# Two graph attention layers on one core: layer 1's turned matrix split between TensorE and transposing DMAs

## Chip, core and metric

One Trainium2 chip, one of its cores. The metric is the device time of one execution in microseconds, as the median of the runs shown. The inputs are x (4096 x 128, fp32), an adjacency matrix of 4096 x 4096 int32 with about 0.2% of ones, crowded at low indices, and the weights of the two layers.

## What is computed

```python
# layer 0
h = x @ W
e = leaky_relu((h @ a_src)[:, None] + (h @ a_dst)[None, :], 0.2)
valid = (adj > 0) & (h.sum(axis=1) != 0)[None, :]
att = where(valid, softmax(where(valid, e, -1e9), axis=1), 0)
attention = where(att >= 1e-4, att, 0) * valid.sum(axis=1)[:, None]   # and 0 where a row's top is under 1e-4
x = layernorm(x + elu(h + attention @ h))
# layer 1
scores = where(adj > 0, leaky_relu(x @ ks.T, 0.2), -9e15)
x = layernorm(x + softmax(scores, axis=1) @ ks)
```

Both layers are dense over the 4096 x 4096 pairs. Everything but the loads and stores happens on chip.

## The kernel before

The 4096 rows are cut into 32 tiles of 128 rows, one per partition. A tile's row of the attention matrix has 4096 columns, which are 32 blocks of 128 and 4 chunks of 1024. Nodes' features `h_all`, the row `d_all` of destination terms, `zero_cols`, and ks in several forms stay in SBUF for the whole program.

For one tile, layer 0 runs so. VectorE's `mask0` adds `d_all` to a mask (0 or a huge negative number) and takes the row maximum. ScalarE's `bend0` applies the leaky slope and `raise0` the exponential with its sum, in two halves. VectorE's `cut` zeroes what is below the threshold. TensorE's `turn0` transposes the 32 blocks into PSUM (L290), ScalarE's `copy0` brings them to `att0T`, and `sum0` multiplies them with `h_all` in fp32 (L410). `residual0`, `elu_exp`, `elu` and `normalise0` give the tile x1 of 128 x 128. `turn_q` transposes it (L444) and `q_high_part` and `q_low_part` split it in two fp16 parts.

Layer 1 then: `score` (L381, L382, L386) makes the products of the fp16 parts of q and ks, `bend1` the leaky slope into `att1`, `mask1` adds the mask and takes the maximum, `raise1` the exponential. `turn1` transposes all 32 blocks on TensorE (L290 again). ScalarE's `copy1` writes their fp16 high part, scaled by 1024, to `high1T` (L687), and VectorE's `low_part1` what is left, also fp16, to `low1T` (L996). `sum1` multiplies both with the fp16 parts of ks and a column of ones: two matmuls per block, 257 and 129 columns wide (L438, L439):

```python
pe.matmul(acc, high1T[:, part], k_parts[:, k, 0:2 * D + 1], start=(k == 0), stop=False)
mm = pe.matmul(acc[:, D:], low1T[:, part], k_parts[:, k, D:2 * D + 1], start=False, stop=(k == BLOCKS - 1))
```

`finish1` divides by the sum (L1003), adds the two products (L1005, L1008), and `normalise1` ends the tile.

Masks: POOL's queue loads each adjacency tile twice, with a cast from int32 to bf16. `load_adj` (L1325) fills one of three `mask` buffers for layer 1. For layer 0, SP's queue copies `zero_cols` into one of two `mask_zero` buffers (`lay_zeros`, L265) and `add_adj` (L1329) adds the adjacency tile to it in flight. `build_mask` (L889) and `zero_mask` (L899) turn both into masks.

PSUM has three places of 1024 columns (`work`) that scores and turned blocks share in a fixed rotation, and two banks for the sums. Each engine has its own queue, and its order is written out by hand as a list per slot: slot t holds layer 0's sums of tile t, the turn and part of the sums of layer 1 for tile t-1, and the scores of tile t; `to_first_slot`, `first_slot`, `early_slots` and `last_slots` are the start and the end. Semaphores alone tie the engines together.

## Time and profile before

| | |
|---|---|
| median of 3 runs | 857.0 us (856.76 to 857.24) |
| span of the profiled execution | 855.3 us |
| busy: TensorE / VectorE / ScalarE / POOL | 827.0 / 788.1 / 760.6 / 224.9 us |
| packets of the DMA queues of POOL / SP | 66.06 MB / 38.80 MB |

The profile is of one execution, and its page gives the span, from the first to the last instruction, as that execution's time; it has no second figure. Busy time is the time in which at least one instruction of the engine runs. Matmuls are pipelined, so the duration of one is longer than the distance to the next; what one costs is read from the distances.

### The profile page before, as it was taken

How to read it: one execution, taken by the hardware profiler on the slowest of the kernel's cores; microseconds unless marked ns; L12 is line 12 of the kernel's file. 1: busy time of each engine (PE TensorE's matmuls, PEld its weight loads, DVE VectorE, ACT ScalarE, POOL GpSimd, SP SyncE). 2: the span in 40 equal slices, each digit the busy share in tenths (PEclk: the TensorE clock that was granted, in tenths of full speed). 3: DMA queues.
4: the chain of work that ended last, by engine and by line, in shares of the span. 5: the costliest groups of instructions: out<-in, count | busy, mean ns of one | idle time of the engine just before them, and what ended most of it. 6: DMA issues, size and time to landing. Idle time of an engine off the chain costs nothing.

```text
span 855.3 us, 17732 instructions
## 1 busy us (share of the span) xinstructions
PE 827.0 (97%) x7139; PEld 714.2 (84%) x7139; DVE 788.1 (92%) x1009; ACT 760.6 (89%) x732; POOL 224.9 (26%) x446
## 2 busy tenths in 40 slices
PE   7489999999999999999999999999999999999997
PEld 7468888888998888889888888988888898888876
DVE  3999999999999999999999999999999999997865
ACT  2899999999999999999999999999999999998763
POOL 2033232323312233332223333222233321222100
PEclk9799999999999999999999999999999999999999
DMA  9999786666688766668866667886666678611000
GB/s 212 239 131 172 151 149 102 122 130 131 141 155 148 106 120 130 132 139 154 151 104 122 130 131 139 153 153 104 126 124 136 135 151 155 103 31 24 13 2 10
DMA packets 39969, 106.07 MB, mean 124 GB/s; under 512 B 11088, under 2 KB 23504, under 8 KB 32208
## 3 DMA queue, kind: packets, MB, share of 16 engines
q0 software_dynamic: 20864, 66.06, 53.5%
q1 hardware_dynamic: 18592, 38.80, 12.7%
q8 instruction: 57, 0.93, 0.4%
q14 instruction: 24, 0.20, 0.1%
q10 hardware_dynamic: 432, 0.07, 0.1%
HBM read 138.48 MB, written 2.10 MB: 164 GB/s over the span
## 4 chain that ended last, share of the span: by engine, by line
PE 83%; DVE 9%; ACT 4%; issue 2%; DMA 1%; POOLq 0%; POOL 0%; ACTq 0%; DVEq 0%
PE work L290 23%; PE sums L410 23%; PE sums L438 12%; PE work L381 6%; PE work L382 6%; PE work L386 6%; PE sums L439 6%; DVE att1T L996 2%; DVE att L908 2%; ACT att L677 1%; ACT att L634 1%; PE sums L444 1%; PE work L315 1%; ACT att L654 1%; ACT att0T L666 1%
## 5 line engine op out<-in xcount | busy, mean ns | idle before, releaser
L290 PE MATMUL work<-ident,att 128*128 128x128 f32 x2072 | 256.2, 275 | 14.0 <-DVE att L1098 12.6
L290 PEld LDWEIGHTS work<-ident,att 128*128 128x128 f32 x2072 | 233.6, 142 | 22.7 <-DVE att L1098 13.0
L410 PE MATMUL sums<-h_all,att0T 128*128 128x128 f32 x2048 | 244.2, 275 | 0.0
L410 PEld LDWEIGHTS sums<-h_all,att0T 128*128 128x128 f32 x2048 | 236.1, 192 | 0.1
L438 PE MATMUL sums<-k_parts,att1T 128*128 128x257 f16 x1024 | 182.3, 274 | 0.3 <-DVE att1T L996 0.2
L439 PE MATMUL sums<-k_parts,att1T 128*128 128x129 f16 x1024 | 177.3, 218 | 0.0
L996 DVE SCALAR_TENSOR_TENSOR att1T<-work,att1T 128x1024 f16<-128x1024 f32 x128 | 152.3, 1209 | 12.9 <-ACT att1T L687 12.8
L687 ACT ACTIVATE att1T<-work 128x1024 f16<-128x1024 f32 x127 | 129.4, 1029 | 27.9 <-PE work L290 27.9
L921 DVE SCALAR_TENSOR_TENSOR att<-att,cut 128x2048 f32<-128x2048 f32 x62 | 145.2, 2346 | 0.0
L672 ACT ACTIVATE att<-work 128x1024 f32<-128x1024 f32 x128 | 127.7, 1028 | 19.5 <-PE work L386 19.5
L960 DVE CUSTOM_DVE_ANT_0 att<-att,mask 128x2048 f32<-128x2048 f32 x62 | 141.3, 2282 | 2.0 <-ACT att L672 2.0
L908 DVE CUSTOM_DVE_ANT_0 att<-mask_zero,d_all 128x4096 f32<-128x4096 bf16 x31 | 137.0, 4420 | 1.7 <-PE work L290 1.7
L666 ACT COPY att0T<-work 128x1024 f32<-128x1024 f32 x128 | 126.7, 1023 | 4.5 <-PE work L290 4.5
L677 ACT ACTIVATE att<-att,bias 128x2048 f32<-128x2048 f32 x62 | 126.0, 2036 | 2.6 <-DVE bias L987 2.6
L654 ACT ACTIVATE att<-att,bias 128x2048 f32<-128x2048 f32 x62 | 124.7, 2011 | 0.0
L634 ACT ACTIVATE att<-att,node_parts 128x4096 f32<-128x4096 f32 x31 | 114.9, 3708 | 0.0
L438 PEld LDWEIGHTS sums<-k_parts,att1T 128*128 128x128 f16 x1024 | 100.3, 98 | 14.2 <-issue 0.4
L439 PEld LDWEIGHTS sums<-k_parts,att1T 128*128 128x128 f16 x1024 | 100.4, 98 | 1.3
L381 PE MATMUL work<-kT,qT 128*128 128x512 f16 x256 | 97.7, 382 | 0.9 <-ACT qT L697 0.7
L382 PE MATMUL work<-kT,qT 128*128 128x512 f16 x256 | 97.8, 382 | 0.0
L1325 POOL DMA_DIRECT2D mask<-adj x31 | 19.3, 622 | 226.6 <-DVE top L960 225.4
L386 PE MATMUL work<-kT,qT 128*128 128x512 f16 x256 | 76.6, 381 | 0.0
(123 smaller groups left out, 669.6 us busy)
## 6 DMA issues: line engine op xcount, KB each, us to landing
mask<-adj POOLq DMA_DIRECT2D x31, 1024.0 KB, 8.6
mask_zero<-zero_cols SPq DMA_DIRECT2D x29, 1024.0 KB, 5.0
mask_zero<-adj POOLq DMA_DIRECT2D x29, 1024.0 KB, 11.7
att<-x SPq DMA_DIRECT2D x4, 512.0 KB, 6.7
k_parts<-ks POOLq DMA_DIRECT2D x2, 1024.0 KB, 19.7
x_sb<-x SPq DMA_DIRECT2D x32, 64.0 KB, 2.8
out<-x SPq DMA_DIRECT2D x32, 64.0 KB, 4.8
mask<-adj POOLq DMA_DIRECT2D x2, 512.0 KB, 6.6
```

Of the source, the lines that this page charges most:

```text
L290: mm = pe.transpose(place[:, b * P:(b + 1) * P], source(c * PER + b), ident[:, :])
L381: pe.matmul(o, qT[:, 0, :], kT[:, 0, part], start=True, stop=False)
L382: pe.matmul(o, qT[:, 0, :], kT[:, 1, part], start=False, stop=False)
L410: mm = pe.matmul(acc0, att0T[:, k * P:(k + 1) * P], h_all[:, k, :], start=(k == 0), stop=(k == BLOCKS - 1))
L438: pe.matmul(acc, high1T[:, part], k_parts[:, k, 0:2 * D + 1], start=(k == 0), stop=False)
L439: mm = pe.matmul(acc[:, D:], low1T[:, part], k_parts[:, k, D:2 * D + 1], start=False, stop=(k == BLOCKS - 1))
L666: nc.scalar.copy(att0T[:, cols(c)], work[:, (1, 2, 0, 1)[c], :]).then_inc(copied0, 1)
L677: nc.scalar.activation(att1[:, half(k)], att1[:, half(k)], ACT.Exp, bias=bias1[u % 2][:, :]).then_inc(exp1, 1)
L908: nc.vector.tensor_tensor_reduce(att0[p][:, :], mask_zero[p][:, :], d_all[:, :], 1.0, -NO_ROW_MAX, ALU.add, ALU.max, top0[p][:, :]).then_i ...
L921: nc.vector.scalar_tensor_tensor(b, b, cut0[p][:, :], b, ALU.is_ge, ALU.mult).then_inc(cut_done, 1)
L960: nc.vector.tensor_tensor_reduce(att1[:, half(k)], att1[:, half(k)], mask[u % MASKS][:, half(k)], 1.0, -3.0e38, ALU.add, ALU.max, top1[u % ...
L996: nc.vector.scalar_tensor_tensor(low1T[:, cols(c)], work[:, (2, 0, 1, 2)[c], :], LIFT, high1T[:, cols(c)], ALU.mult, ALU.subtract).then_in ...
```

## The change

It changes layer 1's turn and sums, the masks, some buffers, and the order of all five queues.

1. Of layer 1's 32 blocks, TensorE turns the first 12 (`WHOLE_BLOCKS`), in two fills of 6. ScalarE copies them in fp32, times 1024, to `whole1T`, and `sum_whole` multiplies them in fp32 with `k_whole`, ks and a column of ones, 129 wide.
2. The other 20 are split where they lie, before any turn: ScalarE's `split_high` writes the fp16 high part to a new buffer `high1`, VectorE's `low_part1` the low part in two pieces of 1280 columns into the tail of `att1`. SP issues three transposing transfers per tile (`turn_high`, `turn_low` twice) into `high1T` and `low1T`. `sum_split` multiplies them, one slot later than the whole ones, with three matmuls per block.
3. The last tile uses no transposing transfer: all its blocks are turned by TensorE.
4. The sums of layer 1 are 129 columns in place of 257, so `finish1` has one product less.
5. One adjacency load per tile, in four buffers. `zero_mask` makes layer 0's mask as a minimum of `mask` and `zero_cols`; `lay_zeros` and `add_adj` go.
6. `raise0` is one exponential over 4096 columns in place of two halves.
7. Smaller buffers are shared (`elu0`, `res1`), x1 has three buffers, and all orders are new; the PSUM places follow a table of fills.

```diff
+FILL_BLOCKS = 6
-MASKS = 3
+MASKS = 4
-            def turn1(u, c, layer0):
-                turn(work[:, (2, 0, 1, 2)[c], :], c, lambda b: att1[:, b * P:(b + 1) * P]).then_inc(turned1, 1)
+            def turn1(u, i):
+                blocks = fill_blocks(i)
...
+            def sum_whole(u, i):
+                pe.wait_ge(copied1, 2 * u + i + 1)
...
+                for k in fill_blocks(i):
+                    mm = pe.matmul(acc1, whole1T[:, k * P:(k + 1) * P], k_whole[:, k, :], start=(k == 0), stop=False)
...
+            def split_sum(blocks):
+                for b in blocks:
+                    k = b - WHOLE_BLOCKS
                     part = slice(k * P, (k + 1) * P)
-                    pe.matmul(acc, high1T[:, part], k_parts[:, k, 0:2 * D + 1], start=(k == 0), stop=False)
-                    mm = pe.matmul(acc[:, D:], low1T[:, part], k_parts[:, k, D:2 * D + 1], start=False, stop=(k == BLOCKS - 1))
+                    pe.matmul(acc1, high1T[:, part], k_parts[:, k, 0:D + 1], start=False, stop=False)
+                    pe.matmul(acc1[:, 0:D], high1T[:, part], k_parts[:, k, D + 2:], start=False, stop=False)
+                    mm = pe.matmul(acc1, low1T[:, part], k_parts[:, k, 0:D + 1], start=False, stop=(b == BLOCKS - 1))
...
+            def sum_split(u, i):
...
+                if i == 0:
+                    pe.wait_ge(high_turned, 16 * (u + 1))
+                pe.wait_ge(low_turned[i], 16 * (u + 1))
...
+            def turn_high(u):
+                sp.wait_ge(high_ready, u + 1)
+                if u > 0:
+                    sp.wait_ge(summed1, 4 * u)
...
+                sp.dma_start_transpose(high1T.rearrange("p (b r) -> p b r", r=P), high1[:, :]).then_inc(high_turned, 16)
+            def turn_low(u, i):
+                sp.wait_ge(low1, 2 * u + (1 if i == 1 else 2))
...
+                sp.dma_start_transpose(low1T[:, piece(i)].rearrange("p (b r) -> p b r", r=P),
+                                       att1_halves[:, low_at(i)]).then_inc(low_turned[i], 16)
...
             def slot(t):
-                if t + 4 < TILES:
-                    lay_zeros(t + 4)
...
+                store(t - 4)
+                load_x(t + 1)
+                turn_low(t - 1, 1)
+                turn_low(t - 1, 0)
+                turn_high(t - 1)
...
             def bend1(u, c):
                 act.wait_ge(scored, 4 * u + c + 1)
...
+                    for i in range(2):
+                        if low_at(i).start < 2 * (c + 1) * CHUNK and low_at(i).stop > 2 * c * CHUNK:
+                            act.wait_ge(low_turned[i], 16 * u)
...
+            def split_high(u):
+                act.wait_ge(exp1, 2 * u + 2)
+                if u > 0:
+                    act.wait_ge(high_turned, 16 * u)
+                nc.scalar.activation(high1[:, :], att1[:, WHOLE_COLS:N], ACT.Copy, scale=LIFT).then_inc(high_ready, 1)
...
-                    nc.vector.tensor_scalar(m, m, 0.0, -NO_EDGE, ALU.is_le, ALU.mult).then_inc(zero_masked, 1)
+                nc.vector.tensor_tensor(mask_zero[:, :], mask[f % MASKS][:, :], zero_cols[:, :],
+                                        ALU.min).then_inc(zero_masked, 1)
...
-            def low_part1(u, c):
+            def low_part1(u, i):
+                dve.wait_ge(high_ready, u + 1)
+                if i == 0:
+                    dve.wait_ge(low1, 2 * u + 1)
+                nc.vector.scalar_tensor_tensor(att1_halves[:, low_at(i)], att1[:, piece_cols(i)], LIFT, high1[:, piece(i)],
                                                ALU.mult, ALU.subtract).then_inc(low1, 1)
...
-                    pe.wait_ge(kT_low, c + 2)
+                if t == 0:
+                    pe.wait_ge(kT_low, CHUNKS)
```

How the orders move, at three places of a slot in the middle of the program. In the rows a name without its buffer number stands for the buffer, x8 for eight of the same kind in a row.

TensorE before: layer 0's turns and sums with layer 1's turns between them, then layer 1's sums in pairs (16 blocks, of which two are shown).

```order
L290 MATMUL work<-ident,att_1 128x128 x24
L410 MATMUL sums<-h_all,att0T 128x128 x8
L290 MATMUL work<-ident,att_1 128x128 x8
L410 MATMUL sums<-h_all,att0T 128x128 x16
L290 MATMUL work<-ident,att 128x128 x8
L410 MATMUL sums<-h_all,att0T 128x128 x8
L290 MATMUL work<-ident,att 128x128 x8
L438 MATMUL sums<-k_parts,att1T 128x257
L439 MATMUL sums<-k_parts,att1T 128x129
L438 MATMUL sums<-k_parts,att1T 128x257
L439 MATMUL sums<-k_parts,att1T 128x129
```

TensorE in the change, from layer 0 to the split sums (L391 is `turn0`, L518 `sum0`, L528 `turn1`, L547 to L549 one block of `split_sum`), and below it from the second fill of `turn1` to the next scores (L540 is `sum_whole`, L566 `turn_q`, L494 `score`).

```order
L391 MATMUL work<-ident,att_1 128x128 x32
L518 MATMUL sums<-h_all,att0T 128x128 x32
L528 MATMUL work<-ident,att 128x128 x6
L547 MATMUL sums<-k_parts,att1T 128x129
L548 MATMUL sums<-k_parts,att1T 128x128
L549 MATMUL sums<-k_parts,att1T 128x129
L547 MATMUL sums<-k_parts,att1T 128x129
```

```order
L528 MATMUL work<-ident,att 128x128 x6
L540 MATMUL sums<-k_whole,att1T 128x129 x6
L566 MATMUL sums<-ident,x_0 128x128
L540 MATMUL sums<-k_whole,att1T 128x129 x6
L494 MATMUL work<-kT,qT 128x512
```

Layer 0 stands in one piece, `turn1` has 12 blocks in place of 32, and the split sums of the tile before stand between its two halves; the second half of the whole sums comes behind the turn of q and ahead of the scores.

ScalarE before, from `bend0` (L634) over the cast of q (L697) and one half of `raise0` (L654) to the four `bend1` (L672):

```order
L634 ACTIVATE att_1,absent<-att_1,node_parts 128x4096
L687 ACTIVATE att1T<-work 128x1024
L697 CAST qT<-sums 128x128
L687 ACTIVATE att1T<-work 128x1024
L654 ACTIVATE att_1,z<-att_1,bias 128x2048
L672 ACTIVATE att<-work 128x1024 x4
L666 COPY att0T<-work 128x1024
L654 ACTIVATE att_1,z<-att_1,bias 128x2048
L666 COPY att0T<-work 128x1024 x2
```

and in the change (L893 is `elu_exp`, L820 `bend0`, L876 `copy1`, L899 the cast of q, L840 `raise0`, L863 `bend1`, L851 `copy0`):

```order
L893 ACTIVATE elu<-elu 128x128
L820 ACTIVATE att_0,absent<-att_0,node_parts 128x4096
L876 ACTIVATE att1T<-work 128x768
L899 CAST qT<-sums 128x128
L840 ACTIVATE att_0,z<-att_0,bias 128x4096
L863 ACTIVATE att<-work 128x1024 x4
L851 COPY att0T<-work 128x1024 x4
L868 ACTIVATE att<-att,bias 128x1536
```

The exponential of layer 0 stands whole between the cast of q and the four bends, and the four copies of layer 0 follow in one piece.

VectorE before, from a low part (L996) over `elu` (L937 to L944) and `finish1` (L1003 to L1013) to `normalise0` (L951):

```order
L996 SCALAR_TENSOR_TENSOR att1T<-work,att1T 128x1024
L937 TENSOR_TENSOR low<-y_exp,x_sb 128x128
L939 SCALAR_TENSOR_TENSOR res<-y,low 128x128
L942 BN_STATS stat<-res 128x6
L944 BN_AGGR mv<-stat 128x2
L1003 RECIPROCAL rz<-sums 128x1
L1005 SCALAR_TENSOR_TENSOR res_half<-sums,rz,x 128x128
L1008 SCALAR_TENSOR_TENSOR res<-sums,rz,res_half 128x128
L1011 BN_STATS stat<-res 128x6
L1013 BN_AGGR mv<-stat 128x2
L996 SCALAR_TENSOR_TENSOR att1T<-work,att1T 128x1024
L951 TENSOR_SCALAR x<-res,mv,rstd 128x128
```

and in the change (L1243 is a low piece, L1193 to L1200 `elu`, L1256 to L1265 `finish1`, L1207 `normalise0`, L1212 the low part of q):

```order
L1243 SCALAR_TENSOR_TENSOR att<-att,high 128x1280
L1193 TENSOR_TENSOR elu<-elu,x_sb 128x128
L1195 SCALAR_TENSOR_TENSOR elu<-y,elu 128x128
L1198 BN_STATS stat<-elu 128x6
L1200 BN_AGGR mv<-stat 128x2
L1256 RECIPROCAL rz<-sums 128x1
L1260 SCALAR_TENSOR_TENSOR res<-sums,rz,x_1 128x128
L1263 BN_STATS stat<-res 128x6
L1265 BN_AGGR mv<-stat 128x2
L1207 TENSOR_SCALAR x_0<-elu,mv,rstd 128x128
L1243 SCALAR_TENSOR_TENSOR att<-att,high 128x1280
L1212 TENSOR_TENSOR qT<-sums,qT 128x128
```

The low pieces are two of 1280 columns and read SBUF; one stands ahead of `elu` as before, the other behind `normalise0`, and `finish1` has lost a row.

## Rows read from the trace of the kernel before

**Rows 1.** The page: the span, and the group of L410.

```profile
span 855.3 us, 17732 instructions
...
L410 PE MATMUL sums<-h_all,att0T 128*128 128x128 f32 x2048 | 244.2, 275 | 0.0
```

**Rows 2.** Table by stretch: PE, PEld, DVE, ACT, POOL busy, clock, DMA share, GB/s.

```profile
407.00:432.00 25.00, 25.00 (x220) 21.61 (x218) 24.13 (x31) 23.34 (x23) 7.04 (x16) 1.00 0.72 133
```

**Rows 3.** Chain in order of time (start, duration, work): one slot.

```profile
307.30 0.22 PE work L381
...
312.48 2.62 PE work L290 x24
315.10 1.79 PE sums L410 x16
...
324.87 0.11 PE sums L438
...
327.56 1.75 PE work L290 x16
...
332.18 0.22 PE work L381
```

**Rows 4.** The same chain at the start: fp32 of 131 columns, 2-byte transposes.

```profile
14.31 1.34 PE work L315 x12
...
17.87 0.46 PE sums L327 x8
```

**Rows 5.** VectorE by line, 207 to 705 us: busy, mean ns, idle before and its releaser.

```profile
L996 DVE SCALAR_TENSOR_TENSOR att1T<-work,att1T 128x1024 f16<-128x1024 f32 x81 | 96.2, 1208 | 0.0
L921 DVE SCALAR_TENSOR_TENSOR att<-att,cut 128x2048 f32<-128x2048 f32 x40 | 93.8, 2346 | 0.0
...
L899 DVE TENSOR_SCALAR mask_zero<-mask_zero 128x4096 bf16<-128x4096 bf16 x20 | 24.4, 1218 | 0.0
...
L1005 DVE SCALAR_TENSOR_TENSOR res_half<-sums,rz,x 128x128 f32<-128x128 f32 x20 | 7.0, 351 | 0.7
...
L937 DVE TENSOR_TENSOR low<-y_exp,x_sb 128x128 f32<-128x128 f32 x20 | 5.8, 292 | 6.3 <-ACT y_exp L691 6.3
...
L1003 DVE RECIPROCAL rz<-sums 128x1 f32<-128x1 f32 x20 | 3.4, 168 | 5.5 <-PE sums L439 5.5
```

**Rows 6.** VectorE by line, 0 to 107 us.

```profile
L1098 DVE SCALAR_TENSOR_TENSOR att<-att,cut 128x1024 f32<-128x1024 f32 x4 | 5.0, 1280 | 0.0
...
L896 DVE TENSOR_TENSOR mask_zero<-mask,zero_cols 128x4096 bf16<-128x4096 bf16 x2 | 4.6, 2284 | 0.0
```

**Rows 7.** ScalarE by line, 207 to 705 us.

```profile
L687 ACT ACTIVATE att1T<-work 128x1024 f16<-128x1024 f32 x81 | 83.2, 1028 | 20.6 <-PE work L290 20.6
...
L654 ACT ACTIVATE att<-att,bias 128x2048 f32<-128x2048 f32 x40 | 80.3, 2008 | 0.0
```

**Rows 8.** ScalarE by line, 0 to 107 us.

```profile
L648 ACT ACTIVATE att<-att,bias 128x4096 f32<-128x4096 f32 x1 | 3.7, 3707 | 0.0
```

**Rows 9.** Timeline of all engines: the turn of q and its cast.

```profile
405.12 0.33 PE L444 MATMUL sums<-ident,x 128*128 128x128 f32 x1
...
405.48 0.27 ACT L697 CAST qT<-sums 128x128 f16<-128x128 f32 x1
```

**Rows 10.** DMA issues by line, with median us from issue to landing.

```profile
mask_zero<-zero_cols SPq DMA_DIRECT2D x29, 1024.0 KB, 5.0
...
x_sb<-x SPq DMA_DIRECT2D x32, 64.0 KB, 2.8
...
att1T<-ks SPq DMA_DIRECT2D x1, 0.5 KB, 17.3
```

**Rows 11.** VectorE's timeline: low part of q (L956), last of kT (L1060).

```profile
57.48 0.29 DVE L956 TENSOR_TENSOR qT<-sums,qT 128x128 f16<-128x128 f32 x1 [0.72 <-ACT qT L697]
...
58.94 1.21 DVE L1060 TENSOR_TENSOR kT<-work,kT 128x1024 f16<-128x1024 f32 x1
...
106.86 0.28 DVE L956 TENSOR_TENSOR qT<-sums,qT 128x128 f16<-128x128 f32 x1
```

More of the change, by code:

```diff
@@ L1412 @@
+            first_slots()
+            for t in range(5, TILES - 5):
+                slot(t)
+            last_slots()
 def kernel(x, adj, L0_gnn_W, L0_gnn_a, L1_gnn_ks):
```

1070 lines of the change are left out of this document (671 added, 399 removed).

## The prediction

> **What bounds the kernel now.** I read the page first, for the span and the costliest groups [rows 1]; then the table by stretch, to see whether the middle repeats; then the chain in order of time over one slot, to price TensorE's work; then VectorE and ScalarE by line; last the DMA issues. The table shows three stretches of 25 us, 200 us apart, alike to a hundredth, of which the middle one stands here: TensorE 25.00 busy, VectorE 24.13, ScalarE 23.34, clock 1.00, DMA share 0.72 [rows 2]. So this is one slot per row tile, 32 times, with a start and an end; TensorE is full and two others are close behind. A slot runs from the first score matmul at 307.30 to the next tile's at 332.18: 24.88 us [rows 3]. The change is worth what it takes from the slowest engine, times about 30, and which engine is slowest must be asked again afterwards: VectorE has only 0.87 us idle in 25, ScalarE 1.66.
>
> Matmuls overlap (the page's mean of 275 ns [rows 1] is no price), so I price from starts in the chain. 24 transposes take 2.62 us: 0.109 each. Sixteen rows of L410 take 1.79: 0.112 each, and L410 has 2048 rows for 1024 matmuls, so a fp32 matmul of 128 columns is two of them, 0.223 [rows 1, 3]. L315, fp32 and 131 wide, takes 1.34 for 12, also 0.112 [rows 4]. From 324.87 to 327.56 TensorE does 16 blocks of the fp16 sums (L438 with 257 columns, L439 with 129): 0.168 per block [rows 3]. Eight 2-byte transposes of 128 columns, each with a new weight, take 0.46: 0.0575 each [rows 4].
>
> **TensorE.** Scores, layer 0 and the turn of q stay. A block of layer 1 costs 0.109 + 0.168 = 0.277 now. Twelve blocks are turned by TensorE and summed in fp32: 0.109 + 0.223 = 0.332, 0.055 more: +0.66. Twenty lose their transpose: 20 x 0.109 = -2.18. Their sums are three narrow matmuls (129, 128, 129) in place of 257 and 129: a third of 0.168 each would change nothing, three at 0.0575 make 0.173, so 0 to +0.1; I take +0.05. Together -1.47: TensorE needs 23.41 us per slot.
>
> **VectorE.** 24.13 of 25 is 24.01 per slot. The low part was 4 instructions of 1024 columns from PSUM at 1.208 [rows 5]. It becomes 2 of 1280 that read SBUF. That kind of instruction from SBUF takes 1.280 for 1024 columns and 2.346 for 2048 [rows 5, 6], so 1.041 ns a column and 1.547 for 1280: 4.83 becomes 3.09, -1.74. `finish1` loses one of its two products: -0.35 [rows 5]. Layer 0's mask was a tensor_scalar of 1.218 on data that a second adjacency load brought; it becomes a minimum of two tensors, which the start of this kernel has too, at 2.284 [rows 5, 6]: +1.07. That leaves 22.99 busy. Its idle time is 0.87 per slot, of which 6.3 us in 20 slots (0.31 each) is for the ELU exponential and 5.5 (0.27) for layer 1's sums ahead of the reciprocal [rows 5]. The new order still has a low piece between y_neg and `elu`, now 1.55 long and not 1.21, which covers the first; whether the second goes depends on TensorE. So VectorE needs 23.28 (both gone) to 23.86 (both stay). I take **23.5**, nearer to the end where the wait with a longer cover is gone. It is 0.1 above TensorE: the bound moves to VectorE, or rather all meet.
>
> **ScalarE.** 23.34 of 25 is 23.23 per slot. Layer 0's exponential in one piece is 3.71 in place of 2 x 2.01: -0.31. Layer 1's, as 1536 and 2560 columns, is as long as before. The four copies of 1024 (4.11) become two of 768 (0.82 each, by 0.83 ns a column between 2.008 and 3.707) and the high part of 2560 from SBUF (2.43): -0.04. So 22.9 per slot [rows 7, 8]; its work is covered by the others' 23.5, but not its order (rival A).
>
> **DMA and queues.** Of the adjacency's two loads per tile one goes, and the laying of zeros on SP's queue. The load left has four buffers, so its place comes free a slot earlier than now; I cost it at nothing, covered by that slot. SP gets three transposing transfers per tile, 640 KB for the high halves and 320 KB for each low piece. They start once the split sums of the tile before have read high1T and low1T, and must have landed when the next split sums begin: 23.5 - 3.4 = 20 us later. The low pieces lie in the tail of att1, so ScalarE's third and fourth bend of the next scores wait for them too; counted along TensorE's order they have about 4 and 2.5 us to spare at 3.5 us each. No row shows a transposing transfer. Bounds: SBUF to SBUF, as the zeros, 1 MB in 5.0 us makes 6.3 us of the 1.31 MB; the load of ks in runs of 512 bytes, 2.1 MB in 17.3, is 121 GB/s, and half of that for the 256-byte rows of 128 fp16 values makes 21.6 [rows 10]. I take 8, the lower end and some landing time, because source and target are the memories of the zeros; it is then hidden with 12 us to spare. The x load and the store share SP's queue; a low transpose waits behind a load of x, which waits for `elu`'s first addition, under 1 us after the low piece itself.
> The Trainium skill has two figures that lead apart. Its page VectorE: DVE Perf Modes (the three transpose paths) gives 1309 ns for one 128x128 block by DMA: 40 blocks one after another would be an estimated 52 us per tile, and the sum would come to some 1,700 us. Its page DMA: Bandwidth & Descriptors (latency and other measured facts) gives 261 GB/s for transposing transfers: an estimated 5 us per tile, and the sum stays. No run so far shows which.
>
> **Start and end.** The first scores now wait for all four parts of kT. VectorE makes the last at 58.94 to 60.15, with q's low part done at 57.77 [rows 11]: 2.4 us through which TensorE had scored; but the cuts behind them stand where they stood, so I take half, +1.2, and +0.3 for a mask built a slot earlier less a smaller negation. In the last tile all 32 blocks are turned and 12 summed in fp32: 12 x 0.055 = +0.7, less one product in `finish1`: +0.4.
>
> **The sum.** 31 slots follow the first. Two of the first three show at q's low part, 57.48 to 106.86, a mean of 24.7 [rows 11]; with VectorE at some 24.0: -0.7, three times, -2.1. Then 24 slots at 23.5 - 24.88 = -1.38: -33.1. In the last four VectorE has no masks to build, and TensorE's -1.47 counts: -5.9. With +1.5 and +0.4: -39.2. The profiled execution has a span of 855.3 [rows 1] and no other figure of its own; the median of the three runs, 857.0, is 1.7 above the span. 855.3 - 39.2 + 1.7 = 817.8, so **818**.
>
> **The rivals.**
> A. *ScalarE's order stalls TensorE.* The cast of q starts 0.36 after the turn of q (405.12, 405.48 [rows 9]). Behind it stood half of layer 0's exponential; now the whole stands there, so the first bend ends about 0.36 + 0.17 + 3.9 + 1.0 = 5.4 us after the turn of q. TensorE by then has done six fp32 sums (1.34) and three scores (3.9) and has no free PSUM place for the fourth. I get stalls of 0.1 to 0.6 per slot. At 0.6 on 23.41 the slot is 24.0: 24 x 0.5 = 12 more, **830**. For it: there are three places, each wanted at once. Against: VectorE's 23.5 hides the first 0.1.
> B. *No new wait.* VectorE's two waits go, TensorE alone bounds at 23.41, and the start loses nothing: 24 x 0.1 + 1.5 less, **814**.
> C. *The transposes are late: slower than before.* At the upper bound a tile's three take 21.6 us; with 3.4 of split sums and 1 of landing and semaphores the ring is 26.0 per slot: 27 x 1.12 = 30 more than now, **887**. It decides from 24.88 - 3.4 - 1 = 20.5 us per tile on; from 19 it takes part of the gain. For it: small rows, one queue, and the adjacency load on the same DMA engines. Against: those engines are at 0.72 now [rows 2], and 3 MB of writes per tile become 2.3.
> D. *The time does not move*: split_high makes VectorE's low pieces late and its 0.87 idle grows by what it sheds: **857**.
> E. *The blocks go one by one*, with the skill's 1309 ns beside it. Its price from a row: a whole transfer of 64 KB lands in 2.8 us [rows 10], a ceiling for one block; 40 of them are up to 112 us per tile, the kernel up to 31 x 112 = **3,500**. Against: the zeros, 1 MB in 5.0 us, are far from that.
>
> **How the numbers follow.** Forecast 0.50 (812 to 825), A 0.20, B 0.16, C 0.10, D 0.02, E 0.02. The predicted time is the forecast's. The range takes in B from 811 on, and A up to a full us of stalls, 842; outside are C, D, E and a little of A, 0.16. A measurement of this kernel can tell 0.2% (1.7 us) from no change. Faster 0.86 (forecast, A, B), same 0.02 (D), slower 0.12 (C, E).
>
> **What would show it.** Right: slots of about 23.5; the low piece at about 1.55, the mask at 2.28, the high part at 2.43; VectorE busy over 97% of the middle; transposing transfers that land within 4 us, and nobody waiting for them. Wrong: TensorE idle ahead of the split sums with a DMA as releaser (C, E), or ahead of the fourth score with ScalarE (A); split blocks clearly over 0.173; a start that ends over 3 us later. A slot of 24.88 or more would refute the whole sum.

## The result, and the profile after

The changed kernel takes **862.2 us**, median of 6 runs (859.1 to 863.1), the kernel before beside it 857.1 (854.8 to 857.2): ratio 1.0061, 95% interval 1.0042 to 1.0079. It is slower by half a per cent, where 818 was predicted. (Beside the experiments below the kernel before took 854.6 to 854.9; against that the change is 0.9% slower. Its single runs lie between 853.5 and 857.7.) Its profiled execution took 859.7 us with a span of 857.9, against 855.3 [rows 1].

The page of the changed kernel, span, busy time, the chain that ended last by engine and by line, and one group:

```profile
span 857.9 us, 17717 instructions
...
PE 797.8 (93%) x7159; PEld 688.7 (80%) x7159; DVE 747.9 (87%) x913; ACT 757.3 (88%) x641; POOL 367.5 (43%) x418
...
DVE 36%; POOL 35%; PE 20%; issue 6%; ACT 2%; DMA 1%; POOLq 0%; DVEq 0%; ACTq 0%
DVE att L1177 12%; DVE att L1216 12%; POOL z_sum L1636 12%; PE sums L518 5%; DVE att L1243 4%; POOL gate L1640 4%; POOL var L1658 4%; PE work L391 4%; POOL rz L1638 3%; DVE mask L1147 3%; PE sums L540 3%; POOL rstd L1652 2%; PE work L494 2%; POOL mask L1614 2%; PE work L495 2%
...
L1636 POOL TENSOR_SCALAR z_sum<-z 128x1 f32<-128x1 f32 x31 | 109.5, 3534 | 23.6 <-ACT att L840 21.4
```

All three large engines did what was predicted: each has less to do. Yet the chain runs through POOL for 35% of the time, and 12% is one instruction on 128 numbers, `z_sum`, at 3.53 us each. The table by stretch, against [rows 2]:

```profile
407.00:432.00 25.00, 24.21 (x225) 20.87 (x223) 23.13 (x29) 23.35 (x20) 11.59 (x14) 1.00 0.54 101
```

TensorE went from 25.00 to 24.21 busy, VectorE from 24.13 to 23.13, the DMA share from 0.72 to 0.54, and POOL from 7.04 to 11.59, though its list got shorter. The slot is 24.73 us from one low part of q to the next; it was 24.87. What VectorE waits for over the whole span (total, times, longest):

```profile
DVE x L1207 <- POOL rstd L1652: 25.9, 30, 2.2
...
DVE res L1270 <- POOL rstd L1660: 21.3, 25, 1.7
```

These are two waits for POOL's reciprocal deviations, 47 us in all. The timeline of one slot shows them made. POOL:

```profile
397.58 0.64 POOL L1614 DMA_DIRECT2D mask<-adj  x1 [12.36 <-DVE top L1216]
398.26 1.51 POOL L1658 TENSOR_SCALAR var<-mv 128x1 f32<-128x1 f32 x1
399.85 0.57 POOL L1660 TENSOR_TENSOR rstd<-var,minus_half 128x1 f32<-128x1 f32 x1
...
400.77 4.45 POOL L1636 TENSOR_SCALAR z_sum<-z 128x1 f32<-128x1 f32 x1
...
405.98 1.39 POOL L1640 TENSOR_SCALAR gate<-z_sum,edges 128x1 f32<-128x1 f32 x1
...
409.37 0.57 POOL L1652 TENSOR_TENSOR rstd<-var,minus_half 128x1 f32<-128x1 f32 x1
```

and VectorE beside it:

```profile
397.39 2.29 DVE L1155 TENSOR_TENSOR mask_zero<-mask,zero_cols 128x4096 bf16<-128x4096 bf16 x1
400.45 0.35 DVE L1270 TENSOR_SCALAR res<-res,mv,rstd 128x128 f32<-128x128 f32 x1 [0.77 <-POOL rstd L1660]
400.71 4.42 DVE L1165 CUSTOM_DVE_ANT_0 att<-mask_zero,d_all 128x4096 f32<-128x4096 bf16 x1
...
405.58 1.48 DVE L1243 SCALAR_TENSOR_TENSOR att<-att,high 128x1280 f16<-128x1280 f32 x1
...
409.98 0.35 DVE L1207 TENSOR_SCALAR x<-elu,mv,rstd 128x128 f32<-128x128 f32 x1 [0.86 <-POOL rstd L1652]
```

Three of POOL's instructions end with one of VectorE's: `var` of layer 1 (1.51, 0.22 when free) with the mask's minimum, `z_sum` (4.45, 0.23 when free) with layer 0's mask step L1165 (4.42), `gate` (1.39, 0.31 when free) with the low piece. In the new order layer 1's deviation stands behind the adjacency load, which waits until VectorE is done with that mask, and the coefficient (edges, z_sum, rz, gate, coef) stands ahead of layer 0's offset and deviation. So both deviations are late, by 0.77 and 0.86 us per slot.

The transposes, by contrast, are hidden in the middle, as the prediction has it. Two rows of the DMA issues (median us from issue to landing), and the only wait for them over the whole span (total, times, longest):

```profile
att1T<-att SPq DMA_TRANSPOSE x62, 3.6
...
att1T<-high SPq DMA_TRANSPOSE x31, 5.1
```

```profile
ACT att L863 <- DMA att1T<-att: 3.9, 4, 1.7
```

The low pieces land within the 4 us that the prediction named as a sign of being right, the high halves (640 KB) do not. ScalarE's waits make 3.9 us, and three of the four stand at the end of the program: 1.67 and 0.53 us among the bends of the last tile but one, 1.49 ahead of the last bend.

### The profile page after: what moved, and what is told of

It reads as the page before. It is cut to its first block, busy times and chain, and to the rows that moved or that the text cites. A ratio compares the mean times of both kernels' runs of the same rounds, so it can differ in the third digit from the quotient of the medians.

```text
span 857.9 us, 17717 instructions
## 1 busy us (share of the span) xinstructions
PE 797.8 (93%) x7159; PEld 688.7 (80%) x7159; DVE 747.9 (87%) x913; ACT 757.3 (88%) x641; POOL 367.5 (43%) x418
## 4 chain that ended last, share of the span: by engine, by line
DVE 36%; POOL 35%; PE 20%; issue 6%; ACT 2%; DMA 1%; POOLq 0%; DVEq 0%; ACTq 0%
DVE att L1177 12%; DVE att L1216 12%; POOL z_sum L1636 12%; PE sums L518 5%; DVE att L1243 4%; POOL gate L1640 4%; POOL var L1658 4%; PE work L391 4%; POOL rz L1638 3%; DVE mask L1147 3%; PE sums L540 3%; POOL rstd L1652 2%; PE work L494 2%; POOL mask L1614 2%; PE work L495 2%
## 5 line engine op out<-in xcount | busy, mean ns | idle before, releaser
L518 PE MATMUL sums<-h_all,att0T 128*128 128x128 f32 x2048 | 236.1, 275 | 0.8 <-ACT att0T L851 0.8
L518 PEld LDWEIGHTS sums<-h_all,att0T 128*128 128x128 f32 x2048 | 232.6, 192 | 1.0 <-ACT att0T L851 1.0
L1165 DVE CUSTOM_DVE_ANT_0 att<-mask_zero,d_all 128x4096 f32<-128x4096 bf16 x31 | 137.0, 4420 | 2.3 <-PE work L391 2.1
L863 ACT ACTIVATE att<-work 128x1024 f32<-128x1024 f32 x128 | 124.3, 1024 | 15.3 <-PE work L499 11.0
L391 PE MATMUL work<-ident,att 128*128 128x128 f32 x1048 | 124.7, 277 | 13.3 <-DVE att L1348 12.0
L391 PEld LDWEIGHTS work<-ident,att 128*128 128x128 f32 x1048 | 119.5, 143 | 20.3 <-DVE att L1348 12.3
L851 ACT COPY att0T<-work 128x1024 f32<-128x1024 f32 x128 | 120.8, 1036 | 6.9 <-PE work L391 6.9
L868 ACT ACTIVATE att<-att,bias 128x1536 f32<-128x1536 f32 (+1 forms) x62 | 121.2, 2004 | 3.5 <-DVE bias L1236 0.3
L1636 POOL TENSOR_SCALAR z_sum<-z 128x1 f32<-128x1 f32 x31 | 109.5, 3534 | 23.6 <-ACT att L840 21.4
L840 ACT ACTIVATE att<-att,bias 128x4096 f32<-128x4096 f32 x31 | 115.2, 3717 | 0.3 <-POOL bias L1627 0.3
L540 PE MATMUL sums<-k_whole,att1T 128*128 128x129 f32 x768 | 100.2, 281 | 16.0 <-DVE res L1260 15.7
L820 ACT ACTIVATE att<-att,node_parts 128x4096 f32<-128x4096 f32 x31 | 114.6, 3698 | 0.0
L547 PE MATMUL sums<-k_parts,att1T 128*128 128x129 f16 x640 | 110.8, 219 | 0.0
L548 PE MATMUL sums<-k_parts,att1T 128*128 128x128 f16 x640 | 110.8, 220 | 0.0
L549 PE MATMUL sums<-k_parts,att1T 128*128 128x129 f16 x640 | 110.7, 218 | 0.0
L540 PEld LDWEIGHTS sums<-k_whole,att1T 128*128 128x128 f32 x768 | 93.0, 195 | 21.8 <-issue 21.4
L494 PE MATMUL work<-kT,qT 128*128 128x512 f16 x256 | 98.2, 384 | 1.1 <-DVE qT L1212 0.9
L495 PE MATMUL work<-kT,qT 128*128 128x512 f16 x256 | 98.2, 384 | 0.0
L1243 DVE SCALAR_TENSOR_TENSOR att<-att,high 128x1280 f16<-128x1280 f32 x62 | 91.8, 1481 | 0.0
```

Of the source, the lines that this page charges most:

```text
L391: mm = pe.transpose(into[:, b * P:(b + 1) * P], source(c * PER + b), ident[:, :])
L494: pe.matmul(o, qT[:, 0, :], kT[:, 0, part], start=True, stop=False)
L518: mm = pe.matmul(acc0, att0T[:, k * P:(k + 1) * P], h_all[:, k, :], start=(k == 0), stop=(k == BLOCKS - 1))
L540: mm = pe.matmul(acc1, whole1T[:, k * P:(k + 1) * P], k_whole[:, k, :], start=(k == 0), stop=False)
L851: nc.scalar.copy(att0T[:, cols(c)], place("turn0", t, c)).then_inc(copied0, 1)
L863: nc.scalar.activation(att1[:, cols(c)], place("score", u, c), ACT.Prelu, alpha=SLOPE).then_inc(bent1, 1)
```

## The experiments

Each is compared with the kernel before, run beside it (854.6 to 854.9 us). "Slot" is the distance of two low parts of q in the middle of the kernel.

### POOL's order in the steady slots

```diff
             def slot(t):
-                deviation0(t - 1)
                 load_adj(t + 3)
-                deviation1(t - 4)
-                coefficient(t + 1)
                 offset0(t + 2)
+                deviation0(t)
+                deviation1(t - 3)
+                coefficient(t + 1)
```

This is the order of the kernel before; `first_slots` and `last_slots` hand over accordingly.

> The changed kernel with one edit: in the 21 steady slots POOL's list is load_adj, offset0, deviation0 of this slot, deviation1, coefficient, where coefficient stood ahead of offset0 and deviation0. Theory P (POOL): VectorE waits 0.86 us per slot for rstd0 and 0.77 for rstd1, because POOL's small operations stand still while VectorE runs an instruction with two SBUF sources (mask0 4.4 us, the low pieces 1.5, the mask minimum 2.3), and z_sum, which stood under mask0 for 4.45 us, is in front of both deviations. With the new list both waits go, a slot falls from 24.73 to 23.4 to 23.7, and the time from 862 to about 836 (832 to 843). Rival S (sum of work): VectorE and ScalarE have the work of 24.7 us once their order is kept, POOL only follows; the slot stays at 24.6 to 24.8 and the time at 860 to 863. Rival D (DMA): the transposing transfers slow POOL's or the others' work; the slot stays too and the small operations stay at their long durations wherever they stand.

Measured: **835.6 us** (834.2 to 839.9), ratio 0.9785 (0.9755 to 0.9815), slot 23.66. Of the two waits 7.6 and 3.5 us are left. POOL's timeline in that kernel:

```profile
399.40 0.23 POOL L1636 TENSOR_SCALAR z_sum<-z 128x1 f32<-128x1 f32 x1
399.71 2.51 POOL L1638 TENSOR_TENSOR rz<-z_sum,minus_one 128x1 f32<-128x1 f32 x1
402.33 2.96 POOL L1640 TENSOR_SCALAR gate<-z_sum,edges 128x1 f32<-128x1 f32 x1
405.40 4.30 POOL L1644 TENSOR_SCALAR coef<-gate,rz 128x1 f32<-128x1 f32 x1
```

and the one wait that VectorE's timeline has left in the slot, for TensorE's split sums:

```profile
420.18 0.17 DVE L1256 RECIPROCAL rz<-sums 128x1 f32<-128x1 f32 x1 [0.56 <-PE sums L549]
```

POOL stands even longer here (busy 17.31 of 25 us), but on the coefficient, which is done at 409.70 and needed at 416.54. So it is not the standing still that costs, but what is queued behind it. By the two ratios (0.9785 and 1.0061) the order of five calls on POOL is worth 2.7%; by the two medians, 862.2 and 835.6, it is 3.1%.

### Which of the two moves

One run brings layer 1's deviation ahead of the load and leaves the coefficient where it is:

```diff
                 deviation0(t - 1)
+                deviation1(t - 4)
                 load_adj(t + 3)
-                deviation1(t - 4)
                 coefficient(t + 1)
                 offset0(t + 2)
```

> Which of the two moves of the POOL list is worth what. In the changed kernel VectorE waits twice per slot for a reciprocal standard deviation of POOL: 0.86 us for layer 0's (the coefficient, whose z_sum and gate stood still under the layer 0 cut and the low piece, is ahead of it on POOL) and 0.77 us for layer 1's (it starts only after the adjacency load, which waits until VectorE is done with the mask, and stands still under the next mask's minimum). Here only layer 1's deviation is moved, from behind the adjacency load to ahead of it, one place in the list; the coefficient stays ahead of the offset. Theory P1 (the late layer 1 deviation is the root: the load, and behind it the coefficient, then start 2.7 us earlier, and the coefficient is through before the offset is due): both waits go, slots 23.6 to 23.8, total 833 to 839. Rival P2 (two separate causes, the coefficient ahead of the offset makes layer 0's wait by itself): only the 0.77 goes, slots about 23.9 to 24.0, total 841 to 846.

The other leaves it behind the load and moves the coefficient last:

```diff
-                deviation0(t - 1)
                 load_adj(t + 3)
                 deviation1(t - 4)
-                coefficient(t + 1)
                 offset0(t + 2)
+                deviation0(t)
+                coefficient(t + 1)
```

> The other half: only the coefficient is moved, behind layer 0's deviation; layer 1's deviation stays behind the adjacency load. Theory P1: layer 0's wait of 0.86 us goes, layer 1's stays at 0.3 to 0.8 us, slots 24.0 to 24.4, total 843 to 854. Rival P2: the 0.86 goes and the 0.77 stays, slots about 23.9, and the gains of this run and the last add up to that of both moves together (26 us). If layer 1's wait costs nothing of its own, the total is that of both moves, about 835.

Measured: **840.7 us** (838.9 to 844.1), ratio 0.9827 (0.9793 to 0.9862), slot 23.87; and **855.1 us** (850.5 to 867.0), ratio 1.000 (0.997 to 1.003). VectorE's timeline, first of the one, then of the other, and last a row of POOL's timeline of the other:

```profile
404.61 0.35 DVE L1207 TENSOR_SCALAR x<-elu,mv,rstd 128x128 f32<-128x128 f32 x1 [0.64 <-POOL rstd L1652]
```

```profile
302.75 0.35 DVE L1270 TENSOR_SCALAR res<-res,mv,rstd 128x128 f32<-128x128 f32 x1 [1.73 <-POOL rstd L1660]
...
401.17 0.35 DVE L1270 TENSOR_SCALAR res<-res,mv,rstd 128x128 f32<-128x128 f32 x1 [0.76 <-POOL rstd L1660]
```

```profile
291.32 7.38 POOL L1640 TENSOR_SCALAR gate<-z_sum,edges 128x1 f32<-128x1 f32 x1
```

Neither theory has it whole. In the first, layer 1's wait goes and 0.64 of the other stays (the total lies between the ranges of P1 and P2). In the second layer 0's goes and layer 1's stays, but in two patterns: slots of 23.90 with 0.76 of waiting, and stretches of slots of 24.85 with 1.73, where `gate` stands 7.38 us under four of VectorE's instructions and holds even the load back. Its runs spread over 17 us. The gains do not add: 0.86 and 0.83 us per slot by themselves (the second in its better pattern), 1.07 together. The reason can be read off. The slot less VectorE's waits is the same each time: 24.73 - 0.86 - 0.77 = 23.10 with the change, 23.87 - 0.64 - 0.11 = 23.12 in the first of the two runs (the 0.11 is for TensorE's sums), 23.90 - 0.76 = 23.14 and 24.85 - 1.73 = 23.12 in the second, and with both moves 23.66 - 0.56 = 23.10, where the 0.56 is the wait for TensorE's sums ahead of the reciprocal. So VectorE needs 23.1 and TensorE 23.66. A first wait for POOL takes the place of that 0.56 and costs only the 0.2 by which it is longer; the second is paid in full.

### The first and last slots too

The same order in `first_slots` and `last_slots`; the last slots, for one:

```diff
             def last_slots():
                 last = TILES - 1
-                deviation0(last - 5)
-                deviation1(last - 8)
                 load_adj(last - 1)
-                coefficient(last - 3)
                 deviation1(last - 7)
-                deviation0(last - 4)
                 offset0(last - 2)
+                deviation0(last - 4)
+                coefficient(last - 3)
```

> The changed kernel with POOL's list in the new order everywhere, the first five and last five slots too. Theory P: on top of the steady slots the third slot (27.5 us, with VectorE waiting 1.7 for rstd1 behind a coefficient that met cut, mask and mask1) comes to about 25, the second to last slots lose 1 to 2 us: 3 to 5 us less than with the steady list alone, about 832. Rival S: nothing beyond noise, 860 to 863.

Measured: **830.7 us** (830.3 to 832.5), ratio 0.9724 (0.9706 to 0.9741), span 828.6, slot 23.66. This is called the mended kernel from here on.

### The wrong order put into the kernel before

Its `coefficient(t + 1)` moved ahead of `offset0(t + 2)`, from slot 3 on.

```diff
+                if t >= 3 and t + 1 < TILES:
+                    coefficient(t + 1)
                 if t + 2 < TILES:
                     offset0(t + 2)
...
-                if t + 1 < TILES:
+                if t < 3:
                     coefficient(t + 1)
```

> The kernel before with one edit: from slot 3 on POOL's coefficient stands ahead of offset0, that is where VectorE runs the cut and mask0, and not behind the deviations. No transposing transfer exists here. Theory P: its small operations stretch to the length of the VectorE instruction that they meet (one of z_sum, the reciprocal or gate takes 2 to 4.4 us in most slots, where the longest mean now is 1.3 us for z_sum), though the time may hardly move (855 to 861), since offset0 has room. Rival D: without transposes they stay as short as now, means of 0.2 to 1.3 us. Rival S says nothing of durations and expects 857.

Measured: **865.4 us** (863.1 to 865.9), ratio 1.012 (1.010 to 1.014). `z_sum` stands 3.58 us there, where it took 1.17, in a kernel without any transposing transfer. So the transfers are not what slows POOL. The time lies 4.4 us above the expected range: 25 middle slots of 24.97 on average for 24.87 make 2.5 us, and two of the last slots, 28.60 and 28.72 for 24.63 and 26.93, another 5.8. TensorE still bounds that kernel's middle, so POOL's standing costs little there. In the first of the two long slots it is a plain wait in POOL's queue: `z_sum` waited 8.23 us, until 780.45, for ScalarE's exponential of the next tile, the deviation stood behind it, and VectorE waited for that:

```profile
784.42 0.34 DVE L951 TENSOR_SCALAR x<-res,mv,rstd 128x128 f32<-128x128 f32 x1 [4.18 <-POOL rstd L1369]
```

### What POOL stands still for

24 instructions that wait for nothing, put on POOL in one slot of the middle, in the mended kernel and in the one before:

```diff
+                if t == 15:
+                    for i in range(24):
+                        nc.gpsimd.tensor_scalar(probe[:, i:i + 1], minus_one[:, :], 1e-30, None, ALU.max)
```

> The disputed cost by itself. The POOL order everywhere (830.7 us), and in one slot of the middle 24 more instructions on POOL, each a tensor_scalar of 128x1 from a constant into a column of its own, which nothing waits for and which wait for nothing. Theory H (POOL stands still while VectorE runs an instruction whose sources all lie in SBUF, whatever its type, and runs free when VectorE is idle, reads PSUM or does its small ones): each probe that meets the fp32 cut (2.35), the layer 1 mask (2.29), the bf16 minimum (2.29), the layer 0 cut (4.42), the bf16 tensor_scalar (1.22) or the low piece (1.48) ends with it, the others take 0.2 to 0.3. Rival W (only instructions with two bf16 or fp32 tensor sources hold POOL): those that meet the bf16 tensor_scalar of 1.22 take 0.2 to 0.3. Rival G (POOL's own wait or the transfers): long and short ones bear no relation to VectorE's instructions. The total may rise by 1 to 8 us, since offset and deviation stand behind the probes once.

> The same 24 probes on POOL in one slot of the kernel before, where VectorE's low part is four instructions of 1.208 us that read PSUM and SBUF, and no transfer transposes. Theory H: probes under a low part take 0.2 to 0.3 us, those under the cuts, the masks and the bf16 tensor_scalar stand until these end. Rival L (any long VectorE instruction holds POOL): those under the low parts stand too. Time: 855 to 863 us.

Measured, one run each: 836.3 us (in it, VectorE waited 5.37 us for the deviation behind the probes) and 855.7. A table of the probes alone in the kernel before, by half microseconds (length, busy time and number of probes in it, clock, DMA share, GB/s), and VectorE's timeline of the same stretches:

```profile
430.50:431.00 0.50, 0.46 (x1) 1.00 0.00 0
...
435.00:435.50 0.50, 0.50 (x1) 1.00 0.90 123
...
440.00:440.50 0.50, 0.50 (x1) 1.00 0.19 42
440.50:441.00 0.50, 0.44 (x2) 1.00 0.07 8
...
446.00:446.50 0.50, 0.40 (x2) 1.00 0.69 262
446.50:447.00 0.50, 0.38 (x3) 1.00 1.17 459
```

```profile
430.02 2.34 DVE L922 SCALAR_TENSOR_TENSOR att<-att,cut 128x2048 f32<-128x2048 f32 x1
432.28 1.22 DVE L900 TENSOR_SCALAR mask_zero<-mask_zero 128x4096 bf16<-128x4096 bf16 x1
433.41 2.28 DVE L961 CUSTOM_DVE_ANT_0 att<-att,mask 128x2048 f32<-128x2048 f32 x1
...
438.34 2.35 DVE L922 SCALAR_TENSOR_TENSOR att<-att,cut 128x2048 f32<-128x2048 f32 x1
440.60 4.42 DVE L909 CUSTOM_DVE_ANT_0 att<-mask_zero,d_all 128x4096 f32<-128x4096 bf16 x1
...
445.56 1.22 DVE L997 SCALAR_TENSOR_TENSOR att1T<-work,att1T 128x1024 f16<-128x1024 f32 x1
```

The first probe began at 430.5 and was alone in all ten half microseconds up to 435.5: 5.23 us, the longest, through a cut, a bf16 tensor_scalar and a layer 1 mask. It is not always held so long: another probe, which met the cut at 438.34, ended at about 440.75, when the mask step that follows had already begun, and only the next one stood through that. So POOL gets in between two of VectorE's instructions in some places and not in others; what decides it is open. Under the old low part, which reads PSUM (`work`), probes take 0.205, and so do they while the DMA moves 262 to 459 GB/s. In the mended kernel a probe stands 4.52 us under layer 0's mask step and 1.3 under the new low piece (439.22 to 440.62), which reads only SBUF. Theory H holds, the rivals W, G and L do not. The Trainium skill's page SBUF — State Buffer (who interferes with whom) has this rule: a VectorE instruction with two SBUF inputs, or in one of its two-port modes, contends with a GpSimd instruction that reads SBUF, and the later one blocks. The trace agrees, down to the old low part. The change thus moved the low part to a form that holds POOL, but the largest stand, 4.4 us, comes from the place of `z_sum`.

### The start

On the changed kernel, then on the mended one: at the start VectorE does `mask0(2)` ahead of the first part of kT (it waited 3.6 us there for ScalarE's copy) and q's low part ahead of the last two parts, ScalarE does `elu_exp(0)` ahead of three of its kT copies and the cast of q ahead of `bend0(2)`, and each score waits only for its own part of kT.

```diff
                 if t == 0:
-                    pe.wait_ge(kT_low, CHUNKS)
+                    pe.wait_ge(kT_low, c + 1)
```

> The changed kernel with the old order at the start only: mask0(2) ahead of the first low part of kT, the ELU exponential ahead of three kT copies on ScalarE, q's low part ahead of the last two parts of kT, and the first scores waiting for their own part of kT alone. VectorE's wait of 3.6 us for ScalarE's first kT copy should go: q's low part at 57.5 to 58.5 us and not at 61.8, the time 3 to 4 us less, about 858.5. If VectorE's or ScalarE's work before the second tile's cuts binds instead, the gain shows at q and is gone by the second slot: 861 to 862.

> The POOL order everywhere (830.7 us) and the start's edit on top: at the start VectorE does the cut of tile 2 ahead of the first kT part instead of waiting 3.6 us for ScalarE's first copy, ScalarE does the first ELU exponential ahead of three kT copies, and each score waits for its own part of kT. On the changed kernel itself this edit brought q's first low part 1.7 us forward and was given back by the second slot. Theory S1 (it was given back because VectorE's waits for POOL bound the slots that follow; with POOL's order mended the start's gain stays): total 828.5 to 829.5. Rival S2 (the first three slots are bound by something else, TensorE's or ScalarE's work for two tiles and kT, so the gain is given back here too): total within 830 to 832, the first slots longer by what the start won.

Measured: 861.4 us (860.3 to 863.1) and 829.9 (829.4 to 830.4), within a us of the kernels without it, though q's first low part came 1.7 and 3.3 us earlier. These two figures hold chance: VectorE's first mask minimum begins at another time in each profiled run, at 17.8 to 20.4 us, whatever the edit. Counted from there the kernels can be compared:

| | first mask minimum at | to q's first low part | next five slots | the other slots | to the end of VectorE's work |
|---|---|---|---|---|---|
| before | 20.24 | 37.24 | 124.8 | 646.4 | 23.6 |
| change | 19.35 | 42.42 | 127.3 | 640.5 | 25.5 |
| mended | 18.89 | 42.42 | 124.1 | 614.9 | 25.5 |
| change, start's edit | 20.42 | 39.69 | 132.3 | 640.5 | 25.5 |
| mended, start's edit | 18.36 | 39.67 | 127.4 | 614.8 | 25.5 |
| mended, waits filled | 18.13 | 42.43 | 121.0 | 614.9 | 24.3 |
| start's edit, waits filled | 19.25 | 39.51 | 127.5 | 614.8 | 24.4 |
| start's edit, ten blocks | 20.10 | 39.67 | 128.5 | 613.6 | 26.2 |

The last three rows belong to runs further down. The start's edit is worth 2.7 us at q both times, and the next five slots take 5.0 and 3.3 us more: given back, which is S2's mechanism (its range began at 830). A further run had, beside it, `normalise0` ahead of the low piece in slots 1 and 2; slot 1:

```diff
                 residual0(1)
-                low_part1(0, 1)
                 elu(1)
-                low_part1(0, 0)
                 normalise0(1)
-                build_mask(4)
+                low_part1(0, 1)
                 q_low_part(1)
+                low_part1(0, 0)
+                build_mask(4)
```

> What holds the first slots. The POOL order and the start's edit (829.9 us), and in slots 1 and 2 VectorE normalises ahead of the last low piece (in slot 1 ahead of both), so that POOL's var does not start under a low piece and stand 1.39 us, and layer 1's finish comes behind q's low part in slot 2. Theory Y (in slots 1 and 2 TensorE, which has no or half a tile of split sums to do, waits on the chain from y by ELU, POOL's var and x to the turn of q): slot 1 from 28.05 to 25.5 to 26.5 us, slot 2 from 25.06 to 24 to 24.6, total 826 to 828.5. Rival Z (the gain is given back in slots 3 and 4, 26.64 and 23.84 us now, where another chain of two tiles binds): total 829 to 831.

Measured: 830.1 us (829.6 to 833.4), ratio 0.970 (0.9678 to 0.9721). That is rival Z's number and not its mechanism: slot 1 took 28.56 us where it had taken 28.05. One thing that holds the first slots shows in the clock. Table of 60 to 65 us, of the mended kernel:

```profile
60.00:65.00 5.00, 3.78 (x9) 1.35 (x10) 5.00 (x6) 4.30 (x6) 0.00 (x0) 0.50 0.01 2
```

TensorE had waited 5.4 us for x, and its first scores ran at a granted clock of 0.50 (1.2 GHz); the stretch of 85 to 90 us, after its next wait for x, has 0.66. So the waits were filled with work whose result is overwritten, once on the mended kernel and once with the start's edit too (there 24, 32 and 14 transposes):

```diff
             def turn_q(t):
+                if t < 3:
+                    pe.wait_ge(q_high, t)
+                    pe.wait_ge(q_low, t)
+                    pe.wait_ge(y_ready, t + 1)
+                    for i in range((40, 34, 14)[t]):
+                        pe.transpose(qT_ps, ident[:, :], ident[:, :])
                 pe.wait_ge(x1_ready, t + 1)
```

> What else of the predicted gain is missing with the POOL order mended (830.7 against 818) lies mostly in the start and the first three slots, where TensorE waits for x three times and the granted clock is 0.50 to 0.91 after two of the waits. Here TensorE passes the time of these three waits with 40, 34 and 14 transposes of the identity into q's place, whose results are overwritten, so that only the clock changes. Theory C (the clock after a wait costs): granted clock near 1.00 from 60 to 70 and from 85 to 90 us, first scores at full speed, total 2 to 5 us under 830.7, that is 826 to 829. Rival N (the chain of VectorE and ScalarE binds these slots, and the faster matmuls only wait longer): the clock is near 1.00 and the total within 1 us of 830.7, the first slots unchanged in sum.

> The same with the start's edit (829.9 us): 24, 32 and 14 transposes. There q's first low part was 3.3 us earlier and the sum of the first slots 3.5 us longer, with a granted clock of 0.61 from 60 to 65, 0.72 from 85 to 90 and 0.67 from 110 to 115. Theory C: what the start won was lost to the clock; full speed gives 3 to 6 us, total 824 to 827. Rival N: within 1 us of 829.9.

Measured: **825.5 us** (825.2 to 827.1), ratio 0.9653 (0.9632 to 0.9673), the best version of the study; and 829.9 (828.3 to 830.2). The same row of the first:

```profile
60.00:65.00 5.00, 4.06 (x19) 1.76 (x20) 5.00 (x5) 5.00 (x5) 0.00 (x0) 1.00 0.00 2
```

The clock is 1.00, and slots 1 and 2 went from 25.83 and 25.43 to 23.91 and 23.76 us, 3.6 in all, of which later slots gave back 0.5. Theory C's mechanism holds for the mended kernel, but not all of the 5 us is the clock's: by the table above 3.1 us come in the first five slots and 0.8 from the chance of the start, and 1.2 come at the end, where both filled runs are without the wait for a transposing transfer ahead of the last bend that the eleven other profiles of the changed kernel have (1.30 to 2.50 us). Nothing was edited there, and why the transfer landed in time is open. With the start's edit the filling is worth nothing, which is rival N's number: the clock was full again until 65 us, but slot 1 became 30.9 us. TensorE waited 4.1 us for ScalarE's bend of the scores, which stands behind other work there, and went on at 0.64.

### Ten whole blocks in place of twelve

With the start's edit, and with the early normalisation too:

```diff
-FILL_BLOCKS = 6
+FILL_BLOCKS = 5
```

> As the last, and 10 blocks of layer 1 by TensorE and fp32 sums, 22 split (5 and 11 per piece for 6 and 10). By the prices of the prediction a block that goes over saves TensorE 0.332 and costs 0.173, so two of them give TensorE -0.32 us per slot, VectorE +0.27 (256 more columns of low piece), ScalarE about 0. Theory T (with POOL's order mended TensorE bounds: it is busy 24.92 of 25 us): slots 23.66 become 23.35 to 23.5, total 4 to 7 us under the last run, until VectorE's work and its wait for the sums meet it. Rival V (VectorE bounds, with 22.9 busy and 0.56 of waiting for sums): slots 23.8 to 23.95, total 4 to 7 us over the last run.

> The last one with 10 whole and 22 split blocks. With 12 and 20 and the start's edit, 10 and 22 had slots of 23.58 for 23.65 us in the middle, and lost 5 us in slots 2 to 4. If these are held by the same chain as in the last run's theory Y: 1 to 2 us under the last run. If VectorE's longer low pieces hold them: 1 to 4 us over it.

Measured: 833.1 us (832.6 to 833.4) and 833.1 (830.6 to 834.9), 3 over their partners and in neither range. The slot did shrink, from 23.66 to 23.58, half of theory T's least: VectorE, with 0.27 more work, then waits only 0.3 for the sums, so all three engines meet. The 3 us are not shown to be the blocks' cost: in the table above, counted from the first mask minimum, the first of the two runs gains 1.3 us in the middle, loses 1.1 in the first five slots and 0.7 at the end (ScalarE's waits for a transpose went from 3.8 to 7.6 us), 0.5 in all, and began 1.7 us later by chance.

## Why the prediction was wrong

**The step that failed.** The prediction priced TensorE, VectorE, ScalarE and the DMA, and nothing on POOL. POOL's 7.04 busy in 25 us [rows 2] stands in its rows, and no term came of it. VectorE's step "needs 23.28 (both gone) to 23.86 (both stay)" knew only the two waits that the kernel before had; the change moved `coefficient` and `deviation1` on POOL's list, and what was queued behind them there was not followed. The two new waits are 0.86 and 0.77 us. The prediction asked which engine is slowest afterwards, and of ScalarE's new order whom it stalls (rival A); of POOL's list neither was asked. The trace of the kernel before had a sign of it, `z_sum` at 1.31 us under `build_mask` on VectorE, next to `var` of the same kind at 0.23:

```profile
405.05 1.31 POOL L1352 TENSOR_SCALAR z_sum<-z 128x1 f32<-128x1 f32 x1
```

```profile
404.98 1.22 DVE L889 TENSOR_SCALAR mask<-mask 128x4096 bf16<-128x4096 bf16 x1
```

**Point by point.**
- TensorE 23.41: the slot is 23.66 where it binds, so -1.47 came out as -1.22. The matmuls were priced right (a split block comes to 0.170 for the 0.173 taken); the missing 0.25 stands ahead of and in the first six whole sums, which take 1.58 us where the second six take 1.34. Waits for the mended kernel's weight loads, 300 to 600 us (total, times, longest), 0.28 each time ahead of the first whole sum:

```profile
PEld sums L540 <- issue: 3.7, 13, 0.3
```

- VectorE's work: 22.99 was predicted, 22.86 of a slot of 24.73 measured; low piece 1.48 for 1.55, mask minimum 2.29 for 2.28. With its small gaps 23.1, under the predicted floor. The first wait (the ELU exponential) went as said; the second grew to 0.56 once POOL was mended, and is TensorE's bound seen from VectorE.
- ScalarE 22.9: 23.08 in a slot, high part 2.34 for 2.43. Rival A's stall of the fourth score shows in no middle slot; with the start's edit the first slot has it once, 1.4 us, and 4.1 when filled.
- DMA, 8 us for the three, hidden in 20: one after another their landing times would make 12.3, and nobody waits in the middle; the end is another matter (below). Rivals C and E fell. Of the two figures of the Trainium skill that led apart, the 261 GB/s of DMA: Bandwidth & Descriptors (latency and other measured facts) makes an estimated 2.5 us for the 640 KB, which landed in 5.1; the 1309 ns per block of VectorE: DVE Perf Modes (the three transpose paths) makes an estimated 26 us for its 20 blocks, if they went one by one. The trace is nearer the first.
- Rival D came nearest in time (857, with a chance of 0.02), and by luck: VectorE's idle time did grow by about what it shed, from 0.87 to 1.87 per slot, but behind POOL; split_high did not make the low pieces late.
- Start +1.5: q's first low part came at 61.77, 4.3 later than the 57.48 before [rows 11], and 5.2 counted from the first mask minimum, since VectorE waited 3.6 for ScalarE's first part of kT, which the order had put in its way; and TensorE came out of the wait at half clock. End +0.4: from the last low part of q to the end it took 28.3 against 26.7, so +1.6. The difference is the 1.49 us that ScalarE waited for a transposing transfer ahead of the last bend; in the filled run, which has no such wait, it took 27.2, so +0.5.

**The sum, closed.** In spans, the prediction is 855.3 - 39.2 = 816.1. From 857.9: POOL's order -29.3 (828.6), the run with filled waits another -4.9 (823.7), of which some 3 are the clock in the first slots. Of the 7.6 us left, 24 middle slots of 23.66 for 23.5 make 3.8 and the first q at 60.56 for 58.7 makes 1.9; the other 1.9 is spread over first and last slots. As this run also began 2.1 us earlier than the profile of before (first mask minimum at 18.13 for 20.24), the start is missed by 4.0.

So the change's arithmetic was sound: with a fitting order on POOL it takes 2.8% off the kernel, and 3.5% in the run with the first waits filled. The order it came with gives that back on an engine that is busy 43% of the time.

## What to carry to other kernels

When an edit moves work, write out the list of every engine, the idle ones too, and ask for each entry what it may stand behind; a short instruction on POOL costs what VectorE's instruction beside it costs. Put first on such a queue what a busy engine waits for, and last what is needed late. A wait that replaces another is free up to the old one's length, so two causes need not add; measure them alone and together. Before a difference of 1 or 2 us between two profiles is put down to an edit, count from an event that the edit can't move. Where TensorE waits for some us at the start, look at the granted clock behind the wait before moving the work ahead of it.

## What the runs showed of the hardware

- A POOL instruction on 128x1 numbers (0.2 us) that meets a long VectorE instruction on SBUF alone stands until that one ends (4.45 us under one of 4.42), and in some places through the ones behind it: 5.23 us through three, 7.38 through four. In others it gets in between two that follow each other (a probe ended at about 440.75, between the cut from 438.34 and the mask step from 440.60).
- It can work the other way: with a load's issue on POOL under way (1.96 us for 1.26), the bf16 tensor_scalar beside it took 1.49 us for 1.22, in the kernel before with the moved coefficient.
- After a wait of TensorE of 5.4 us the granted clock was 0.50 in the 5 us that followed, and filling the wait with transposes kept it at 1.00; slots 1 and 2 were 3.6 us shorter with it.
- One transposing transfer of 320 KB from SBUF to SBUF lands in 3.6 us and one of 640 KB in 5.1 (medians), and the issue holds SP's queue for 1.3 and 3.2 us (medians of 62 and 31).
